# Sparse message passing on one core: in the first edge pass, source numbers come back from memory as rows and VectorE makes two of three one-hots

## The reference

```python
row, col = edge_index
h = jnp.concatenate([x[row], edge_attr], axis=1)
h = jnp.maximum(h @ W1a + b1a, 0.0) @ W1b + b1b
ssum = jax.ops.segment_sum(h, col, num_segments=x.shape[0])
```

## Time and profile before

| | us |
|---|---|
| median of 3 runs | 3633.37 (3633.12 to 3634.44) |
| the profiled execution's own time | 3635.56 |
| its span in the trace | 3633.8 |
| first look-up of the pass to the last message's sum | 1774.9 to 2202.8 |
| busy over the span: PE, DVE, ACT, POOL | 2789.7, 2949.4, 1525.8, 1358.0 |
| DVE idle before `ep_sums` L1461, ended by PE L1641 | 51.9, of it 49.5 |

### The profile page before, as it was taken

The page is one execution under the profiler, slowest core; times in us unless marked ns, Lnnn a source line. Parts: engine busy times, 40 slices in busy tenths (PEclk is TensorE's granted clock), DMA queues, the critical chain, the costliest instruction groups (busy, mean ns, idle before and its releaser), DMA issues. The chain is left out here.

```text
span 3633.8 us, 77596 instructions
## 1 busy us (share of the span) xinstructions
PE 2789.7 (77%) x25482; PEld 2031.7 (56%) x25482; DVE 2949.4 (81%) x6844; ACT 1525.8 (42%) x3073; POOL 1358.0 (37%) x1260
## 2 busy tenths in 40 slices
PE   2098989970474376177699997899999699979994
PEld 1065666640122022022699996466666699969994
DVE  9899999979698998999677774655554799968887
ACT  2455655650352253154699994333333200022221
POOL 0066666651686375286000000455554000024440
PEclk9999999985797698599799998999999699989997
DMA  8978777774796496398477661322222243324441
GB/s 286 418 231 221 219 199 214 213 208 153 220 296 195 128 295 216 94 294 258 146 218 226 217 210 38 76 67 68 68 67 56 56 109 105 96 69 110 115 110 35
DMA packets 449003, 601.16 MB, mean 165 GB/s; under 512 B 84997, under 2 KB 333635, under 8 KB 448621
## 3 DMA queue, kind: packets, MB, share of 16 engines
q1 hardware_dynamic: 402817, 505.88, 45.8%
q0 software_dynamic: 39424, 78.61, 7.2%
q10 hardware_dynamic: 6380, 11.77, 1.1%
HBM read 359.53 MB, written 230.75 MB: 162 GB/s over the span
## 5 line engine op out<-in xcount | busy, mean ns | idle before, releaser
L1211 PE MATMUL psum<-a_probs,z 128*65 128x512 f32 (+1 forms) x1050 | 438.7, 557 | 156.7 <-DVE a_probs L1107 156.7
L1850 DVE TENSOR_SCALAR rp_hot_dst<-rp_ramp,slot_key 128x696 bf16<-128x696 f16 x900 | 300.2, 403 | 221.8 <-PE psum L1994 221.8
L907 POOL DMA_INDIRECT slots<-bc_rec,idx x400 | 388.1, 970 | 211.4 <-issue 107.2
L605 POOL DMA_INDIRECT slots<-h,idx x256 | 344.2, 1345 | 303.0 <-DMA h<-recs 232.8
L1143 ACT ACTIVATE a_tops<-a_tops,a_s_low 128x512 f32<-128x512 f32 (+2 forms) x300 | 283.4, 946 | 296.4 <-DVE a_tops L1098 285.3
L1211 PEld LDWEIGHTS psum<-a_probs,z 128*65 128x65 f32 x1050 | 122.7, 140 | 468.2 <-DVE a_probs L1107 302.9
L1827 POOL DMA_INDIRECT rp_fetch<-piece_rows,slot_row x283 | 279.0, 986 | 240.6 <-PE psum L1994 183.2
L1107 DVE SCALAR_TENSOR_TENSOR a_probs<-a_tops,a_counts 128x512 f32<-128x512 f32 (+2 forms) x300 | 288.8, 964 | 34.6 <-issue 22.5
L1098 DVE SCALAR_TENSOR_TENSOR a_tops<-table,a_s_rest,big 128x512 f32<-128x512 f32 (+2 forms) x300 | 306.4, 1024 | 3.9 <-DMA big<-shift_rows 3.1
L1922 ACT ACTIVATE rp_msg<-psum 128x192 bf16<-128x192 f32 (+1 forms) x456 | 176.1, 386 | 303.4 <-PE psum L1968 298.8
L1985 PE MATMUL psum<-rp_hot_dst,rp_msg 128*128 128x512 bf16 x1234 | 258.2, 313 | 2.6 <-ACT rp_by_relation L1933 1.4
(11 more groups left out here) (461 smaller groups left out, 6753.4 us busy)
## 6 DMA issues: line engine op xcount, KB each, us to landing
slots<-big SPq DMA_DIRECT2D x60, 1012.5 KB
ep_rec<-slots SPq DMA_DIRECT2D x60, 1012.5 KB, 5.8
a_counts<-edge_counts SPq DMA_DIRECT2D x75, 538.5 KB, 4.4
a_counts<-edge_counts SPq DMA_DIRECT2D x150, 256.0 KB, 4.5
a_counts<-edge_counts SPq DMA_DIRECT2D x75, 512.0 KB
edge_counts<-bc_counts SPq DMA_DIRECT2D x12, 3125.0 KB
hot_rows<-ep_hot_src SPq DMA_DIRECT2D x300, 96.0 KB
sp_hot_src<-hot_rows SPq DMA_DIRECT2D x300, 96.0 KB
```

The lines of the kernel that those rows point to most:

```text
L605: pool.indirect_dma_start(k.slots, bass.IndirectOffsetOnAxis(k.idx[:, at:at + 1], 0), self.rows[y][:, t, :], None).then_inc(self.scattered ...
L907: pool.indirect_dma_start(k.slots, bass.IndirectOffsetOnAxis(k.idx[:, first + t:first + t + 1], 0), rec[:, j, t, :], None).then_inc(scatte ...
L1211: last = nc.tensor.matmul(sums[:, a:b], k.z[:, s, 0:D + 1], probs[:, a:b], start=s == 0, stop=True, skip_group_check=True)
L1850: v.tensor_scalar(hot_dst[:, q % HOT_SLOTS, :], ramp[:, :], k.slot_key[:, q:q + 1], None, ALU.is_equal)\
```

## The change

In the first edge pass:

- DVE still cuts out `slot_lo`, now four batches ahead from the fifth batch on. PE turns the 15 columns of a batch with one matmul (`turn_lo`) to 15 x 128. ACT copies them to SBUF (`copy_lo`). POOL's queue writes them to DRAM as 1920 fp16 numbers (`lo_rows`, 3840 bytes), waits for that, waits for the one-hots of three batches before, and reads the row back to all 128 partitions (`spread_lo`, 480 KB), into one of 3 places in `k.big`.
- The one-hot of chunks c with c % 3 == 2 is made on ACT as before, with square and relu, from SBUF (`raise_source`). The other 200 are made on DVE by one comparison (`match_source`, fp16 to bf16). Both are made 5 chunks ahead (`HOT_AHEAD`).
- The 900 matmuls of `spell` go. `RECORD_LOADS` is 6 in place of 5, so SP loads batch b after `message` of chunk 5(b-5)-1, and stores the 5 one-hots from 5(b-5) behind it.
- `node_sums` stands on POOL behind the first five `spread_lo`.

```diff
+    LOADS, READ_AHEAD, FIRST_READ = Ring.RECORD_LOADS, 4, 3
+    HOT_AHEAD, LOOK_AHEAD = 5, 3
+    LO_SLOTS, BATCHES = 3, NCHUNK // FILL
+    READ_AT = {b: (b - READ_AHEAD) * FILL for b in range(READ_AHEAD + 1, BATCHES)}
+    READ_AT.update({FIRST_READ: 1, READ_AHEAD: 3})
+    raised_here = lambda c: c % 3 == 2
...
+        def wait_hot_free(eng, c):
+            if c >= HOT_SLOTS:
+                eng.wait_ge(looked_up, c - HOT_SLOTS + 1)
+                eng.wait_ge(hot_io[c % HOT_SLOTS], 16 * (c // HOT_SLOTS))
...
+                def spread_lo(b):
+                    pool.wait_ge(lo_copied, b + 1)
+                    nc.gpsimd.dma_start(k.lo_rows[b, :].rearrange("(t p) -> t p", p=P), lo_t[:, b % 2, :]).then_inc(lo_kept, 16)
+                    pool.wait_ge(lo_kept, 16 * (b + 1))
+                    if b >= LO_SLOTS:
+                        last = (b - LO_SLOTS + 1) * FILL - 1
+                        pool.wait_ge(hot_matched, matched_to(last))
+                        pool.wait_ge(hot_raised, raised_to(last))
+                    nc.gpsimd.dma_start(lo_all[:, b % LO_SLOTS, :], k.lo_rows[b, :].partition_broadcast(P))\
+                        .then_inc(lo_in[b % LO_SLOTS], 16)
...
+                def match_source(c):
+                    wait_lo(dve, c)
+                    wait_hot_free(dve, c)
+                    v.tensor_scalar(hot_src[:, c % HOT_SLOTS, :], lo_chunk(c), k.lane[:, 0:1], None, ALU.is_equal)\
+                        .then_inc(hot_matched, 1)
...
                 for c in range(NCHUNK):
-                    if edges and c % FILL == 0 and c // FILL + READ_AHEAD < NCHUNK // FILL:
-                        describe(c // FILL + READ_AHEAD)
+                    if edges and c in READ_IN:
+                        describe(READ_IN[c])
+                    if edges and c + HOT_AHEAD < NCHUNK and not raised_here(c + HOT_AHEAD):
+                        match_source(c + HOT_AHEAD)
                     hot_target(c)
...
-                    if edges and 0 <= ahead < NCHUNK:
-                        square_key(ahead)
-                    if edges and 0 <= ahead - 1 < NCHUNK:
-                        hot_source(ahead - 1)
+                        if c - 1 in READ_IN:
+                            copy_lo(READ_IN[c - 1])
+                        if c + HOT_AHEAD < NCHUNK and raised_here(c + HOT_AHEAD):
+                            raise_source(c + HOT_AHEAD)
...
-                for c in range(-SPELL_AHEAD, NCHUNK):
-                    if KEY_BANKS and c + SPELL_AHEAD < NCHUNK:
-                        spell(c + SPELL_AHEAD)
-                    if 0 <= c + LOOK_AHEAD < NCHUNK:
+                for c in range(-LOOK_AHEAD, NCHUNK):
+                    if c + LOOK_AHEAD < NCHUNK:
                         look_up(c + LOOK_AHEAD)
                     if c >= 0:
                         add_up(c)
+                    if edges and c in READ_IN:
+                        turn_lo(READ_IN[c])
...
-    FIRST_RECORDS, RECORD_LOADS, HOT_SLOTS = 3, 5, 8
+    FIRST_RECORDS, RECORD_LOADS, HOT_SLOTS = 3, 6, 8
```

More of the change, by code:

```diff
@@ L1268, in edge_pass @@
     nc = k.nc
-    LOADS, READ_AHEAD = Ring.RECORD_LOADS, 3
-    SPELL_AHEAD, LOOK_AHEAD = 6, 3
+    LOADS, READ_AHEAD, FIRST_READ = Ring.RECORD_LOADS, 4, 3
+    HOT_AHEAD, LOOK_AHEAD = 5, 3
+    edges = kind == "edges"
+    LO_SLOTS, BATCHES = 3, NCHUNK // FILL
+    READ_AT = {b: (b - READ_AHEAD) * FILL for b in range(READ_AHEAD + 1, BATCHES)}
+    READ_AT.update({FIRST_READ: 1, READ_AHEAD: 3})
+    READ_IN = {c: b for b, c in READ_AT.items()}
+    raised_here = lambda c: c % 3 == 2
+    RAISED = [c for c in range(NCHUNK) if raised_here(c)]
+    MATCHED = [c for c in range(NCHUNK) if not raised_here(c)]
+    raised_to = lambda c: sum(x <= c for x in RAISED)
+    matched_to = lambda c: sum(x <= c for x in MATCHED)
     DST_SLOTS, MSG_SLOTS, SUM_SLOTS, HOT_SLOTS = 4, 4, 3, Ring.HOT_SLOTS
-    edges = kind == "edges"
     FETCHES = edge_fetches(kind)
@@ L1280, in edge_pass @@
         sb = lambda name, shape, dt=FP32: ctx.enter_context(nc.sbuf_tensor(f"{tag}_{name}", shape, dt))
-        described, spelled, hot_made, looked_up = sem("described"), sem("spelled"), sem("hot_made"), sem("looked_up")
+        described, hot_matched, hot_raised, looked_up = sem("described"), sem("hot_matched"), sem("hot_raised"), sem("looked_up")
+        lo_turned, lo_copied, lo_kept = sem("lo_turned"), sem("lo_copied"), sem("lo_kept")
+        lo_in = [sem(f"lo_in{y}") for y in range(LO_SLOTS)] if edges else []
         rows_taken, msg_made, dst_made = sem("rows_taken"), sem("msg_made"), sem("dst_made")
@@ L1391, in _ @@
             def _(pool):
+                def spread_lo(b):
[8 more added lines that the diff above has]
+                        .then_inc(lo_in[b % LO_SLOTS], 16)
+                if edges:
+                    for b in range(READ_AHEAD + 1):
+                        spread_lo(b)
                 if aside:
@@ L1397, in _ @@
                                         bass.IndirectOffsetOnAxis(left_no[:, 0:1], 0)).then_inc(left_rows, 16)
+                if edges:
+                    for b in range(READ_AHEAD + 1, BATCHES):
+                        spread_lo(b)
                 if kind == "near" and FETCHES:
@@ L1513, in _ @@
                 if edges:
-                    for b in range(READ_AHEAD):
+                    for b in range(FIRST_READ):
                         describe(b)
@@ L1517, in _ @@
                 left_number()
+                if edges:
+                    for c in range(HOT_AHEAD):
+                        if not raised_here(c):
+                            match_source(c)
                 if kind == "near":
@@ L1601, in _ @@
                         act.dma_start(k.term_rows.rearrange("(t p) f -> p t f", p=P), k.table[:, :, :]).then_inc(terms_in, 16)
-                for c in range(-SPELL_AHEAD, NCHUNK):
+                if edges:
+                    for b in range(FIRST_READ):
+                        copy_lo(b)
+                    for c in range(HOT_AHEAD):
+                        if raised_here(c):
+                            raise_source(c)
+                for c in range(NCHUNK):
                     if c in FETCH_NO:
                         weigh_fetched(c)
-                    ahead = c + SPELL_AHEAD - 1
-                    if edges and c >= 0:
+                    if edges:
                         rectify(c)
-                    if edges and 0 <= ahead < NCHUNK:
-                        square_key(ahead)
-                    if edges and 0 <= ahead - 1 < NCHUNK:
-                        hot_source(ahead - 1)
+                        if c - 1 in READ_IN:
+                            copy_lo(READ_IN[c - 1])
+                        if c + HOT_AHEAD < NCHUNK and raised_here(c + HOT_AHEAD):
+                            raise_source(c + HOT_AHEAD)
                     if c % NT == 1 and c > NT:
@@ L1620, in _, with turn_lo @@
             def _(pe):
[L1621 to L1629 removed]
+                def turn_lo(b):
+                    pe.wait_ge(described, b + 1)
+                    if b >= KEY_BANKS:
+                        pe.wait_ge(lo_copied, b - KEY_BANKS + 1)
+                    nc.tensor.matmul(turned_bank(b), k.slot_lo[:, b * FILL * SLOTS:(b + 1) * FILL * SLOTS], k.ident16[:, :],
+                                     start=True, stop=True).then_inc(lo_turned, 1)
                 def look_up(c):
                     if edges:
[L1633 removed]
+                        wait_hot(pe, c)
                     else:
@@ L1658, in add_up @@
                     last.then_inc(added, 1)
-                for c in range(-SPELL_AHEAD, NCHUNK):
-                    if KEY_BANKS and c + SPELL_AHEAD < NCHUNK:
-                        spell(c + SPELL_AHEAD)
-                    if 0 <= c + LOOK_AHEAD < NCHUNK:
+                if edges:
+                    for b in range(FIRST_READ):
+                        turn_lo(b)
+                for c in range(-LOOK_AHEAD, NCHUNK):
+                    if c + LOOK_AHEAD < NCHUNK:
                         look_up(c + LOOK_AHEAD)
```

57 lines of the change are left out of this document (32 added, 25 removed).

## The result

| | before | changed |
|---|---|---|
| median of the runs, us | 3633.9 (3633.12 to 3638.52, 4 runs) | 3794.3 (3789.8 to 3805.52, 4 runs) |
| ratio, 95% interval | 1 | 1.0442 (1.0427 to 1.0457) |
| profiled execution, us | 3635.56 | 3791.51 |
| its span, us | 3633.8 | 3789.4 |

The change costs 160 us; 3775 was predicted. The pass can be cut by instructions that both kernels have: the first record load that SP issues inside the pass, the ends of messages 4, 269 and 299 on DVE (called T5, T270 and T300, as in the prediction), and the first instruction of the next stage.

The account below looks back on a forecast made before the run. PE and ACT were taken as full before; in the changed kernel a DVE-store-load loop would bound the pass. Loop with placements +141, last chunks -4, start +5, sum +142 on the median 3633.37: 3775 us, range 3700 to 3830.

Parts of the forecast that it names:

- The wait and its loop: DVE's comparison waits for a store behind SP's load, which DVE's messages release; 9.0 us a batch, chance 0.58.
- A lap: One batch from load to load: 5.8 load, 0.28 store, 1.1 added transfer, 1.8 on DVE, together 9.0 us.
- B: Rival: the loop holds but the spread transfer costs nothing; 7.9 us a batch, 3716 us, chance 0.17.
- Its sign: Test on SP's record loads: landing at about 7 us supports the forecast, still at 5.8 supports B.
- DVE's part: DVE's work in a batch after the store lands: 1.35, 1.90 or 2.14 us by chunk, mean 1.80.
- Placements: In every fifth batch SP issues 5 placements ahead of the load, 3.91 us inside the loop, 10 times: 39 us.
- The last chunks: The pass's last 25 chunks store without a load ahead and go at PE's pace, 0.16 faster each: -4 us.
- The start: At the pass's start source numbers cross memory twice, competing with three loads: +5 us, bounds 0 and 10.
- PE: PE loses 900 matmuls and gains one a batch at 0.01 a chunk: 1.24 us a chunk, 6.2 a batch.
- rival A: PE's pace decides the pass, as the store lands in time or DVE isn't held: 3590 us, chance 0.06.
- The clock: PE's clock stays near 1.0 in the pass; it decides only where its mean is under 0.69.
- C: Rival: the loop is longer through late loads and the full 1.39 transfer; 9.7 us a batch, 3813 us, chance 0.15.

Follow-up runs that it names:

- Ring of 16: Changed kernel with 16 places in place of 8 in the one-hot ring of the first edge pass; 3676.45 us, ratio to before 1.0101.
- the moved comparison: Changed kernel with DVE's comparison put behind the message and one-hots made 4 chunks ahead in place of 5; 3676.09 us, ratio to before 1.0112.
- the 16 lanes: Changed kernel with the numbers spread to 16 of 128 lanes from the fourth batch on, output wrong; 3759.23 us, ratio to before 1.0346.
- the experiment: Changed kernel with SP issuing placements of finished sums behind the batch's load and stores; 3918.85 us on a second chip, ratio to before there 1.0301.
- stores first: Changed kernel with SP's order stores, load, placements, and 7 places for records, 9 for one-hots; 3643.39 us, ratio to before 0.9994.

## Why the prediction was right

The direction, the mechanism and some 90% of the size were as predicted (142 of 155.6 us on the span). That the sum of the loop came within 4 us is in part luck, as the terms under it show. By its steps:

- **The wait and its loop.** As forecast: 51 waits (some 54 said) at `ep_hot_src` on DVE for the store, and SP's next load at the end of the first or second message behind them. The waits were forecast at 1.5 to 3.5 us, and much more behind the placements; they are 3.3 on average, and 8.2 there. The pass takes 574 us, about 570 said. Ring of 16 and the moved comparison each undo the wait by other means and give back 118 to 125 us.
- **A lap.** To the first store 5.8 + 0.28 + 1.1 = 7.18 was predicted, and the mean is 7.01. But the spread doesn't cost 1.1 in each lap: it costs some 1.6 in 33 laps and nothing in 21. The prediction had it issued close to the load in every batch, since it waits for a one-hot that DVE compares early; in every third batch that one-hot is ACT's and is made later. B, where the spread costs nothing, is excluded by the 16 lanes. Its sign was badly chosen: the median load still lands at 5.9 (1800 to 2160), where the prediction said about 7, and only the mean of the two groups shows the cost. DVE's part is 2.14 in the 43 laps without placements, predicted 1.80. Of the 0.34, the semaphore's step is 0.13, the last message's end 0.08 (it takes 0.56, and 0.48 was counted), SP's issue 0.03, and 0.08 comes from the laps in which ACT makes chunk 5k+8: there the next store lands 0.53 us later, not 0.28. The two errors, -0.17 and +0.34, cancel in part: 9.16 measured, 9.0 predicted.
- **Placements.** 39 predicted, (12.82 - 9.16) x 10 = 37 measured, and 46 to 60 by the experiment, with its noise.
- **The count.** Between T5 and T270 there are 53 laps, in the prediction 54. 53 x 9.16 + 37 = 522, the 522.1 of the table. So the lap's 0.16 too little and the one lap too many cancel: 485 measured, 486 predicted.
- **The last chunks.** -4 predicted, -0.5 measured, since one more lap with a load ends in them; without the loop they take 36.2, -5.4.
- **The start.** +5 predicted in bounds 0 to 10, +7.3 measured. DVE's first comparison waits 10.1 us for the numbers, and a second, 2.5, for those of the next batch.
- **The end.** Nothing predicted; +7.7 measured. This is the one term that I didn't have. I had counted GpSimd's DMAs by what they move and how they delay others, not what it costs that they were on that queue.
- **PE.** 1.24 a chunk predicted, 1.23 measured, but the turn 0.26 and not 0.06. It hides behind the loop here, and would have made rival A about 3603 in place of 3590.
- **The clock.** I said near 1.0; it was 0.84 to 0.91 in the windows above, where PE was busy for 0.71 to 0.79. The loop sets the pace and PE has slack, so the slower clock should cost little; that is argued, and no run measured it. C's late loads did not come: the median of all 60 landings is 6.2, the longest 10.6, against 5.8 and 10.5 before.

The sum was +142 on the span, and +155.6 was measured: the end 7.7, the last chunks 3.5, the loop 3.4 and the start 2.3 more, less 3.3 outside the pass.

## What to carry to other kernels

Before an instruction that waits is put on another engine, write down what stands behind it there, and follow whether that work leads back to the DMA it waits for: here DVE's comparison waited for a store, the store stood behind a 1 MB load, and the load was released by DVE. Such a ring doesn't show in the busy times, in which every engine only looks less loaded (PE went from 99% to 76% of the steady part), and it takes only a few more buffers, or the store issued ahead of the load with a place or two more, to open it. And take the gain from the engine that bounds, with its real instructions in place: 48 us by division were 35 on PE, and start and end took half of those.

## What the runs showed of the hardware

- A small store behind a 1 MB load in the same queue waits for the load: 96 KB landed 6.1 us after the load's issue in before (median), where the load itself took 5.8. In the changed kernel it landed after 8.09 where a 480 KB spread was issued beside the load by another engine, and after 5.87 where the same spread was issued 2.35 us later; over all laps 7.63 and 6.05 on average.
- A DMA of 3.8 KB to DRAM took 1.6 to 6.2 us to land in the changed kernel, where the DMA engines' share was 0.67, with a median of 4.3. In stores first, with a share of 0.95, the median was 5.6 and the longest 7.4; half of these writes stood within 0.6 us behind a 480 KB spread on the same queue, so whether the share or that spread delays them isn't separated.
- GpSimd's queue ended its block with a DRAIN of 10.1 us in each of the ten profiles with 120 DMAs on that queue, and of 0.30 in the three with these DMAs on ACT's queue; the end of the pass was 9.5 us shorter. What it depends on (count, kind) wasn't tried.
- A single matmul of another kind between two groups takes 0.26 us of PE's time, although three in a row before took 0.17. In the chunk shown PE stood idle for 0.16 us ahead of it, and its weights' load began only 0.01 us before it; why it came so late isn't shown.
- ACT, for 128 x 384: an operation that reads the result of the one just ahead starts 0.71 us after it, one that doesn't 0.46.
